# Constant-matrix multiplies on TensorE in three group normalisations and after the first attention

## The chip, the cores and the metric

One core of a Trainium2 chip runs the whole program. The metric is the device time of one execution in microseconds (us), the median of several executions. The engines are TensorE (PE, with its weight loads as PEld), VectorE (DVE), ScalarE (ACT), GpSimd (POOL) and SyncE (SP), which issues the transfers.

## The reference

The input is 8 samples of 256 channels by 32 x 32 positions, in float32. Four blocks follow each other, each added to its input, and each after a group normalisation over 32 groups of channels:

```python
x = x + _L0_conv_ref(_gn(x), ...)   # projections, state-space scans over three resolutions, projection
x = x + _L1_conv_ref(_gn(x), ...)   # attention, 8 heads of 32, over 1024 positions
x = x + _L2_conv_ref(_gn(x), ...)   # dilated depthwise 3x3 convolutions, two 1x1 mixes
x = x + _L3_conv_ref(_gn(x), ...)   # channel norm, attention, channel norm, projection

def _gn(v, G=32, eps=1e-05):
    g = v.reshape(B_, G, C_ // G, H_, W_)
    m = jnp.mean(g, axis=(2, 3, 4), keepdims=True)
    s = jnp.var(g, axis=(2, 3, 4), keepdims=True)
    return ((g - m) / jnp.sqrt(s + eps)).reshape(v.shape)
```

## The kernel before

The kernel is written engine by engine: each engine has its own instruction list, in the order of the source, and semaphores tie the lists together. Nothing reorders them. The channels lie on the partitions in two halves; the 1024 positions are worked in chunks of 512, which fill one PSUM bank of float32 each. All eight banks are one tensor, `PS`.

The samples run one after the other in the loop at the end of the TensorE part. For each of them TensorE does `block0` (block 0, whose last matmuls are on line 1210), `group_norm(b, 1)`, `attention(b, 0)` (its last matmuls are on lines 1301 and 1311, sums of the softmax's rows), `project(b, 0)`, `group_norm(b, 2)`, `block2(b)` (it begins with the depthwise taps of line 1374), `group_norm(b, 3)`, `chan_norm(b, 0)` (channel means of line 1216, channel variances of line 1222), `attention(b, 1)`, and the rest of block 3. The fourth normalisation of a sample, of the next sample's input, is made by `norm_means(b, 4)` and `norm_variances(b, 4)` apart, within the last projection.

A group normalisation goes back and forth between three engines. VectorE takes statistics of each chunk as it is written (line 702) and sums them (line 714). TensorE multiplies the sums by the matrix `g8`, which averages over the 8 channels of a group, into two columns of bank 7 (line 1072). VectorE makes squares of deviations (lines 718 to 727). TensorE multiplies them by `g8` into two columns of bank 6 (line 1076). ScalarE takes logarithm and exponential (lines 429 and 431), VectorE makes the shift (line 731), and VectorE and ScalarE write one half of the normalised `xg` each (lines 734 and 434). TensorE waits for both halves before the next block begins. All these waits are in the TensorE list, so nothing stands in it beside them.

After the first attention TensorE waits for `o_sb(b, 4)`: ScalarE takes the reciprocals of the last rows' sums (lines 605 and 609), and VectorE writes the attention's last outputs into `oT` (lines 973 and 975). Then `linear` (line 1087) makes the projection. Line 1087 is the helper of nearly all 1x1 products, each 128x512 with a 128x128 weight.

A float32 `pe.matmul` shows as two pairs of weight load and MATMUL in the profile. So the 12 products that `attention` makes after a normalisation are 24 records.

`mean128` is a constant 128x128 matrix of 1/128, made once at the start. Bank 5 is in use in the blocks, and nothing in it is live in the normalisations or at the end of the first attention.

Of the kernel before, what the change touches and what calls it, by code (L numbers as in the profile page):

```python
# [23 lines left out]
P = 128  # L24
# [68 lines left out]
def build(nc, x, wpack, vpack, w8, out):  # L93
    with ExitStack() as ctx:
# [18 lines left out]
        mean128 = sb("mean128", [P, P])  # L113
# [23 lines left out]
        PS = ctx.enter_context(nc.psum_tensor("PS", [P, 8, N], F32))  # L137
# [925 lines left out]
        def _(pe):  # L1063
# [3 lines left out]
                pe.matmul(PS[:, s, 0:P], W8[:, s, 0, :], W8[:, s, 1, :], start=True, stop=True).then_inc(folded, 1)  # L1067
            pe.wait_ge(prepared, NPREP)

            def norm_means(b, s):  # L1070
                pe.wait_ge(*gn_sum(b, s + 1))
                pe.matmul(PS[:, 7, 0:2], g8[:, :], msum, start=True, stop=True).then_inc(gn_gm.sem, 1)

            def norm_variances(b, s):
                pe.wait_ge(*gn_m2(b, s + 1))
                pe.matmul(PS[:, 6, 0:2], g8[:, :], m2, start=True, stop=True).then_inc(gn_gv.sem, 1)

            def group_norm(b, s):
                norm_means(b, s)
                norm_variances(b, s)  # L1080
                pe.wait_ge(*gn_xa(b, s + 1))
                pe.wait_ge(*gn_xb(b, s + 1))

# [129 lines left out]
            def chan_norm(b, s, X):  # L1213
                for c in range(NC):
                    for t in range(CT):
                        ins = pe.matmul(PS[:, c, :], mean256[:, :], X[:, t, c * N:c * N + N], start=(t == 0), stop=(t == CT - 1))
                    ins.then_inc(cm_ps.sem, 1)
                for c in range(NC):
                    n = NC * s + c
                    pe.wait_ge(*cm_sq(b, 2 * n + 2))  # L1220
                    for t in range(CT):
                        ins = pe.matmul(PS[:, 2 + c, :], mean256[:, :], sq[:, 2 * c + t, :], start=(t == 0), stop=(t == CT - 1))
                    ins.then_inc(cv_ps.sem, 1)
# [130 lines left out]
            def project(b, a, X, between=None):  # L1354
                for m in range(CT):
                    for c in range(NC):
                        if a == 1 and m == 0:
                            chunk_ready(b, NC + c)
                        if between is not None and m == 0 and c == 1:
                            between()  # L1360
                        if m == 0 and c == 0:
                            pe.wait_ge(*o_raw(b, 4 * a + 4))
                        linear(2 * m + c, w_proj[a], m, X, c, o_ps)

            def block2(b):
                for t in range(2):
                    for c in range(NC):
                        n = 2 * t + c
                        top = c * (HH // NC)
                        for hh, (ky, kx), (y0, y1, x0, x1), first, last in windows(t, c):  # L1370
                            dy, dx = (ky - 1) * RATES[2 * t + hh], (kx - 1) * RATES[2 * t + hh]
                            dst = PS[64 * hh:64 * hh + 64, n, :].rearrange("p (h w) -> p h w", w=WW)[:, y0 - top:y1 - top, x0:x1]
                            src = xg[:, t, :].rearrange("p (h w) -> p h w", w=WW)[:, y0 + dy:y1 + dy, x0 + dx:x1 + dx]
                            ins = pe.matmul(dst, DW[:, t, ky * 3 + kx, 64 * hh:64 * hh + 64], src,  # L1374
                                            start=first, stop=last, skip_group_check=True)
                        ins.then_inc(dw_ps.sem, 1)
                for m in range(2):
                    for c in range(NC):
                        pe.wait_ge(*dw_sb(b, 4))
                        linear(4 + 2 * m + c, MX, m, br, c, mix_ps)  # L1380
                for m in range(2):
                    for c in range(NC):
                        pe.wait_ge(*mix_sb(b, 4))
                        linear(2 * m + c, w_o, m, zm, c, o_ps)

            group_norm(0, 0)
            for b in range(B):
                block0(b)
                group_norm(b, 1)
                attention(b, 0, xg)  # L1390
                pe.wait_ge(*o_sb(b, 4))
                project(b, 0, oT)
                group_norm(b, 2)
                block2(b)
                group_norm(b, 3)
                chan_norm(b, 0, xg)
                attention(b, 1, xg)
                pe.wait_ge(*o_sb(b, 8))
                chan_norm(b, 1, oT)
                norm_means(b, 4)  # L1400
                project(b, 1, oT, lambda: norm_variances(b, 4))
                pe.wait_ge(*gn_xa(b, 5))
                pe.wait_ge(*gn_xb(b, 5))
                pe.wait_ge(*x_new(b, 16))
# [120 lines left out]
```

## Time and profile before

| | |
|---|---|
| Median of 3 runs | 5492.75 us (5491.58 to 5498.53) |
| The profiled execution: its own time | 5495.14 us |
| The profiled execution: its span | 5493.3 us |
| Mean granted TensorE clock over the span | 0.853 |
| TensorE busy | 4249.1 us (77%) |
| VectorE busy | 3607.0 us (66%) |
| ScalarE busy | 2146.6 us (39%) |
| GpSimd busy | 2007.6 us (37%) |

The span runs from the first to the last instruction; 1.8 us of the execution lie outside it. The granted clock is the share of TensorE's full 2.4 GHz that the chip let through: 1.00 is 2.4 GHz, 0.50 is 1.2 GHz, and a number between them over a stretch is a mean of the two levels. A sample takes about 682 us, and the eight are alike but for the places where the clock changes.

### The profile page before, as it was taken

How to read it: one execution, taken by the hardware profiler on the slowest of the kernel's cores; microseconds unless marked ns; L12 is line 12 of the kernel's file. 1: busy time of each engine (PE TensorE's matmuls, PEld its weight loads, DVE VectorE, ACT ScalarE, POOL GpSimd, SP SyncE). 2: the span in 40 equal slices, each digit the busy share in tenths (PEclk: the TensorE clock that was granted, in tenths of full speed). 3: DMA queues.
4: the chain of work that ended last, by engine and by line, in shares of the span. 5: the costliest groups of instructions: out<-in, count | busy, mean ns of one | idle time of the engine just before them, and what ended most of it. 6: DMA issues, size and time to landing. Idle time of an engine off the chain costs nothing.

```text
span 5493.3 us, 44457 instructions
## 1 busy us (share of the span) xinstructions
PE 4249.1 (77%) x16298; PEld 1843.1 (34%) x16298; DVE 3607.0 (66%) x4793; ACT 2146.6 (39%) x2639; POOL 2007.6 (37%) x681
## 2 busy tenths in 40 slices
PE   5688866879668896688866878669796697866978
PEld 2243422434224332243322433224332243322333
DVE  6763677637776368764687646867468674686746
ACT  3233452334423354243542425424254242542524
POOL 3531435404344043440444504434044340443404
PEclk7689977999769997799977999779897798977999
DMA  0020100210002100022000120011200112001020
GB/s 36 0 55 19 29 8 7 48 29 19 8 8 47 34 14 8 9 47 44 3 8 14 41 46 1 8 25 30 46 1 8 31 24 46 1 8 29 19 46 9
DMA packets 62956, 125.75 MB, mean 23 GB/s; under 512 B 18825, under 2 KB 21001, under 8 KB 62482
## 3 DMA queue, kind: packets, MB, share of 16 engines
q1 hardware_dynamic: 62738, 122.91, 9.6%
q8 instruction: 129, 2.11, 0.2%
q14 instruction: 89, 0.73, 0.0%
HBM read 12.23 MB, written 8.39 MB: 4 GB/s over the span
## 4 chain that ended last, share of the span: by engine, by line
PE 47%; DVE 28%; issue 10%; ACT 7%; SPq 4%; POOL 2%; DMA 2%; DVEq 0%; ACTq 0%; POOLq 0%
DVE mx L954 9%; PE PS L1250 8%; PE PS L1292 8%; PE PS L1087 7%; PE PS L1340 7%; PE PS L1374 4%; DVE work L846 3%; DVE work L848 3%; PE PS L1146 3%; PE PS L1184 2%; ACT PT L624 2%; SPq L290 2%; PE PS L1301 2%; SPq L299 2%; POOL work L392 1%
## 5 line engine op out<-in xcount | busy, mean ns | idle before, releaser
L954 DVE TENSOR_REDUCE mx<-PS 128x1 f32<-128x512 f32 x2048 | 1338.1, 687 | 422.0 <-PE PS L1250 417.9
L624 ACT ACTIVATE PT<-PS 128x1024 f32<-128x1024 f32 x1024 | 1006.9, 1023 | 689.9 <-PE PS L1340 660.0
L1250 PE MATMUL PS<-KS,QS 96*128 96x512 f32 x2048 | 894.9, 479 | 195.4 <-DMA KS<-piece 84.7
L408 POOL TENSOR_TENSOR piece<-PT 128x2048 f32<-128x2048 f32 x48 | 220.0, 4584 | 2183.4 <-ACT PT L624 2183.4
L408 POOL TENSOR_TENSOR piece<-piece,PT 128x2048 f32<-128x2048 f32 x192 | 878.0, 4573 | 58.4 <-ACT PT L624 47.1
L388 POOL TENSOR_TENSOR work<-work,Crep 128x1024 f32<-128x1024 f32 x256 | 616.3, 2409 | 390.5 <-DVE work L846 193.1
L1340 PE MATMUL PS<-QS,KS 98*128 98x512 f32 x2048 | 681.4, 424 | 45.9 <-DMA QS<-nm 22.2
L1250 PEld LDWEIGHTS PS<-KS,QS 96*128 96x128 f32 x2048 | 378.0, 197 | 816.2 <-DVE mx L954 578.0
L1292 PE MATMUL PS<-PT,Vt 128*32 128x512 f32 x4096 | 546.0, 605 | 27.0 <-ACT PT L624 27.0
L1184 PE MATMUL PS<-dstk,sel 128*128 128x512 f32 (+1 forms) x640 | 315.7, 568 | 321.1 <-DVE work L848 133.0
L542 ACT ACTIVATE PS<-PS,Aneg 128x1024 f32<-128x1024 f32 x256 | 278.3, 1087 | 628.5 <-PE PS L1184 597.8
L1184 PE MATMUL PS<-ustk,sel 128*128 128x512 f32 (+1 forms) x640 | 335.3, 597 | 182.9 <-DVE work L831 85.6
L1340 PEld LDWEIGHTS PS<-QS,KS 98*128 98x128 f32 x2048 | 376.5, 197 | 291.0 <-ACT PT L624 164.5
L1087 PE MATMUL PS<-xg,W 128*128 128x512 f32 x640 | 354.0, 709 | 81.1 <-ACT Brep L470 36.3
L1184 PEld LDWEIGHTS PS<-dstk,sel 128*128 128x128 f32 x640 | 152.9, 268 | 460.5 <-DVE work L846 178.9
L1184 PEld LDWEIGHTS PS<-ustk,sel 128*128 128x128 f32 x640 | 139.7, 257 | 491.1 <-DVE work L831 170.5
L1146 PE MATMUL PS<-work,ysel 128*32 128x512 f32 (+1 forms) x1536 | 273.1, 802 | 39.3 <-POOL work L392 30.6
L831 DVE TENSOR_TENSOR work<-PS,Brep 128x1024 f32<-128x1024 f32 (+1 forms) x256 | 250.7, 979 | 71.7 <-PE PS L1184 68.8
L946 DVE SCALAR_TENSOR_TENSOR piece<-PS,V,piece 128x1024 fp32r<-128x1024 f32 x64 | 82.2, 1284 | 278.1 <-ACT piece L588 278.1
L392 POOL TENSOR_TENSOR work<-work,Crep 128x640 f32<-128x640 f32 x128 | 210.5, 1648 | 138.7 <-DVE work L857 80.4
L373 POOL TENSOR_TENSOR ustk<-work,ustk 64x1024 fp32r<-64x1024 f32 x16 | 37.6, 2352 | 587.9 <-ACT ustk L485 587.3
L1087 PEld LDWEIGHTS PS<-xg,W 128*128 128x128 f32 x640 | 144.7, 231 | 263.2 <-issue 182.6
(198 smaller groups left out, 4983.0 us busy)
## 6 DMA issues: line engine op xcount, KB each, us to landing
QS<-piece SPq DMA_DIRECT2D x384, 128.0 KB, 2.4
KS<-piece SPq DMA_DIRECT2D x384, 128.0 KB, 2.4
xin<-x SPq DMA_DIRECT2D x8, 1024.0 KB
out<-xr SPq DMA_DIRECT2D x8, 1024.0 KB, 4.0
W<-wpack SPq DMA_DIRECT2D x2, 1024.0 KB
QS<-nm SPq DMA_DIRECT2D x128, 8.0 KB, 1.9
W<-wpack SPq DMA_DIRECT2D x1, 576.0 KB
W<-wpack SPq DMA_DIRECT2D x2, 256.0 KB
```

Source lines behind the costliest of these rows:

```text
L388: pool.tensor_tensor(slot, h, Crep[:, at:at + L], ALU.mult).then_inc(hC_sb.sem, 1)
L392: pool.tensor_tensor(two(slot), two(h), Crep[:, None, at:at + W3].broadcast_to((P, 2, W3)), ALU.mult).then_inc(hC_sb.sem, 1)
L408: pool.tensor_tensor(total, first, PT[:, i % 3, :, :], ALU.add).then_inc(sum_pool.sem, 1)
L542: act.activation(dst, src, ACT.Exp, scale=Aneg[:, ps * SG + g:ps * SG + g + 1]).then_inc(dA_sb.sem, 1)
L624: act.activation(PT[:, i % 3, 2 * pr:2 * pr + 2, :], PS[:, 2 + 2 * pr:4 + 2 * pr, :], ACT.Exp, scale=SCALE).then_inc(p_sb.sem, 1)
L954: dve.tensor_reduce(mx[:, at, cc:cc + 1], PS[:, row_slot(n, cc), :], AX.X, ALU.max).then_inc(r_max.sem, 1)
L1087: ins = pe.matmul(PS[:, bank, :], w[:, k, m * P:m * P + P], X[:, k, c * N:c * N + N], start=(k == 0), stop=(k == CT - 1))
L1146: ins = pe.matmul(PS[32 * j:32 * j + 32, c, 0:N if ps < 2 else W3], ysel[:, q % 4, :], src, start=(q % 4 == 0), stop=(q % 4 == 3), skip_gr ...
L1184: ins = pe.matmul(PS[:, slot + c, 0:wc], sel[:, g % 8, :], stk[:, g // 8, at + c * N:at + c * N + wc], start=True, stop=True)
L1250: pe.matmul(PS[:, row_slot(n, cc), :], QS[0:kd, c, h, q * P:q * P + P], KS[0:kd, h, cc * N:cc * N + N], start=True, stop=True).then_inc(r_ ...
L1292: ins = pe.matmul(PS[32 * j:32 * j + 32, 0, :], Vt[:, kt, DH * h:DH * h + DH], PT[:, i % 3, j, :], start=(kt == 0), stop=(kt == KT - 1), s ...
L1340: ins = pe.matmul(PS[:, 2 + 2 * pr + jj, :], KS[:, h, kt * P:kt * P + P], QS[:, c, h, :], start=True, stop=True)
```

## The change

A helper `keep_busy(count)` issues so many products of `mean128` with itself, 128 columns each, into the first 128 columns of bank 5. Nothing reads them, they wait for nothing and signal nothing. `group_norm` calls it three times, for every normalisation but the very first one: 6 products ahead of the wait for the sums, 4 ahead of the wait for the squares, and 10 ahead of the wait for the normalised `xg`. In the loop over samples there are 18 between the first attention and the wait for its outputs. The loop calls `group_norm` for 1, 2 and 3, so a sample has 3 x 20 + 18 = 78 products, and the kernel 624. The normalisation made by `norm_means(b, 4)` and `norm_variances(b, 4)` has none.

```diff
+            def keep_busy(count):
+
+                for _ in range(count):
+                    pe.matmul(PS[:, 5, 0:P], mean128[:, :], mean128[:, :], start=True, stop=True)
+
...
             def group_norm(b, s):
+                if b + s > 0:
+                    keep_busy(6)
                 norm_means(b, s)
+                if b + s > 0:
+                    keep_busy(4)
                 norm_variances(b, s)
+                if b + s > 0:
+                    keep_busy(10)
                 pe.wait_ge(*gn_xa(b, s + 1))
                 pe.wait_ge(*gn_xb(b, s + 1))
...
                 attention(b, 0, xg)
+                keep_busy(18)
                 pe.wait_ge(*o_sb(b, 4))
                 project(b, 0, oT)
```

The other engines' lists are the same before and after. On TensorE, ahead of the first attention, the list before has the last products of block 0, the two small ones of the normalisation, and the attention's first projections:

```order
L1164 MATMUL PS<-work,mean 128x320 x2
L1210 MATMUL PS<-work,W 128x512 x4
L1072 MATMUL PS<-small,g 128x2
L1076 MATMUL PS<-small,g 128x2
L1087 MATMUL PS<-xg,W 128x512 x12
```

The changed list has at the same place (its lines are numbered 5 to 11 higher; 1073 is `keep_busy`, 1077 and 1081 are the two small products):

```order
L1175 MATMUL PS<-work,mean 128x320 x2
L1221 MATMUL PS<-work,W 128x512 x4
L1073 MATMUL PS<-mean 128x128 x6
L1077 MATMUL PS<-small,g 128x2
L1073 MATMUL PS<-mean 128x128 x4
L1081 MATMUL PS<-small,g 128x2
L1073 MATMUL PS<-mean 128x128 x10
L1098 MATMUL PS<-xg,W 128x512 x12
```

Twenty products now stand between block 0 and the attention, none of them past anything else. On TensorE at the end of the first attention and in the normalisation ahead of block 2, the list before is:

```order
L1311 MATMUL PS<-piece,ones 32x512 x4
L1087 MATMUL PS<-oT,W 128x512 x8
L1072 MATMUL PS<-small,g 128x2
L1076 MATMUL PS<-small,g 128x2
L1374 MATMUL PS<-xg,DW 64x512 x2
```

and the changed one is:

```order
L1322 MATMUL PS<-piece,ones 32x512 x4
L1073 MATMUL PS<-mean 128x128 x18
L1098 MATMUL PS<-oT,W 128x512 x8
L1073 MATMUL PS<-mean 128x128 x6
L1077 MATMUL PS<-small,g 128x2
L1073 MATMUL PS<-mean 128x128 x4
L1081 MATMUL PS<-small,g 128x2
L1073 MATMUL PS<-mean 128x128 x10
L1385 MATMUL PS<-xg,DW 64x512 x2
```

The eighteen stand ahead of the projection, and have to be through before it can begin.

## Rows read from the trace of the kernel before

**Rows 1.** The page's 40 equal slices: granted clock in tenths.
```profile
PEclk7689977999769997799977999779897798977999
```
**Rows 2.** The page's chain that ended last, by engine.
```profile
PE 47%; DVE 28%; issue 10%; ACT 7%; SPq 4%; POOL 2%; DMA 2%; DVEq 0%; ACTq 0%; POOLq 0%
```
**Rows 3.** The chain in order of time, sample 4, first normalisation: start us, us, what.
```profile
2323.24 1.25 ACT xg L434
2324.62 6.20 PE PS L1087 x8
2330.85 1.12 ACT piece L588
...
2333.30 0.69 SPq L290
```
**Rows 4.** The same chain at the third normalisation of that sample.
```profile
2559.58 6.48 PE PS L1216 x8
2566.08 0.70 DVE xg L927
```
**Rows 5.** TensorE in order of time, first normalisation; [idle before <- what ended it].
```profile
2315.79 2.01 PE L1210 MATMUL PS<-work,W 128*128 128x512 f32 x4
2320.73 0.38 PE L1072 MATMUL PS<-small,g 128*128 128x2 f32 x2 [2.94 <-DVE small L714]
2321.97 0.38 PE L1076 MATMUL PS<-small,g 128*128 128x2 f32 x2 [0.86 <-DVE small L727]
2324.62 1.19 PE L1087 MATMUL PS<-xg,W 128*128 128x512 f32 x1 [2.26 <-ACT xg L434]
```
**Rows 6.** The same view, means of the second and of the third normalisation.
```profile
2506.98 0.43 PE L1072 MATMUL PS<-small,g 128*128 128x2 f32 x2 [2.23 <-DVE small L714]
...
2555.27 0.59 PE L1072 MATMUL PS<-small,g 128*128 128x2 f32 x2 [2.99 <-DVE small L714]
```
**Rows 7.** Windows from the first product after normalisation 1: us, PE busy (records), clock, DMA.
```profile
2324.60:2332.60 8.00, 7.98 (x13) 0.68 0.05 6
...
5051.90:5059.90 8.00, 8.00 (x13) 0.68 0.03 3
```
**Rows 8.** The same windows after normalisation 2.
```profile
467.40:475.40 8.00, 7.98 (x28) 0.66 0.00 0
...
2511.10:2519.10 8.00, 7.98 (x34) 0.82 0.01 2
```
**Rows 9.** The same windows after normalisation 3.
```profile
516.90:524.90 8.00, 7.68 (x13) 0.77 0.00 0
...
2559.60:2567.60 8.00, 8.00 (x12) 0.65 0.00 0
```
**Rows 10.** The same windows from the first attention's projection.
```profile
454.20:462.20 8.00, 7.09 (x16) 1.00 0.00 0
...
2495.90:2503.90 8.00, 7.98 (x15) 0.79 0.00 1
```
**Rows 11.** Groups by line, busy us and mean ns: line 1216 after normalisation 3.
```profile
L1216 PE MATMUL PS<-xg,mean 128*128 128x512 f32 x8 | 6.5, 985 | 2.3 <-ACT xg L434 2.3
```
**Rows 12.** Line 1216 at the second attention's end, in the same view.
```profile
L1216 PE MATMUL PS<-oT,mean 128*128 128x512 f32 x8 | 3.7, 605 | 2.6 <-DVE oT L975 2.6
```
**Rows 13.** In order of time, the end of the first attention in sample 4.
```profile
2492.68 0.61 PE L1311 MATMUL PS<-piece,ones 128*32 128x512 f32 x4
...
2495.38 0.49 DVE L975 TENSOR_SCALAR oT<-oT,V 128x512 f32<-128x512 f32 x1
...
2495.92 0.70 PE L1087 MATMUL PS<-oT,W 128*128 128x512 f32 x1 [2.63 <-DVE oT L975]
```
**Rows 14.** TensorE in order of time: short products one behind the other, in block 0.
```profile
1411.44 1.00 PE L1117 MATMUL PS<-f,W 128*128 128x64 f32 x8
1412.28 1.07 PE L1102 MATMUL PS<-f,Wd 128*128 128x512 f32 x2
```
**Rows 15.** The same view, products of 256 columns in an attention.
```profile
2596.48 1.03 PE L1234 MATMUL PS<-W,xg 128*128 128x256 f32 x4
```
**Rows 16.** The same view, the program's first products.
```profile
15.62 1.65 PE L1067 MATMUL PS<-W 8*128 8x128 f32 x6 [15.62 <-DMA W<-wpack]
```

## The prediction, made before the changed kernel ran

> **What bounds the kernel now.** I read the page's slices first. The granted clock is full in few of the 40 slices, and dips again and again [rows 1]. Then the chain of waits: TensorE holds 47% of it, VectorE 28%, no transfer more than a few per cent [rows 2]. So TensorE's speed counts, but only where it stands on the chain. The third view is the chain in order of time at the four places that the change touches. After the first normalisation it goes from ScalarE's half of `xg` straight to TensorE's first eight records of line 1087, and from them over ScalarE and VectorE to SyncE's transfers [rows 3]. After the third one it runs through all eight records of line 1216 into VectorE [rows 4]. After the second one it runs through the depthwise taps. TensorE is the engine that is late at all of them, and whatever it gains there moves the end. In the gaps ahead of them it is idle: 2.94, 0.86 and 2.26 us [rows 5], 2.23 and 2.99 us ahead of the means of the other two [rows 6], 2.63 us at the attention's end [rows 13]. The fourth view, windows of 8 us from the first product after each gap, shows what follows. TensorE is busy for all 8 us, at a mean clock of 0.68, 0.66 to 0.82, and 0.65 to 0.77 [rows 7 to 9]. The clock fell to its 1.2 GHz level during the gap and came back to 2.4 GHz only after some microseconds of work.
>
> **What the slow stretches cost.** In such a window the time lost is (1 - clock) x 8 us, if all of it is TensorE's work.
> - Normalisation 1: the eight windows read 0.65 once and 0.68 or 0.69 seven times [rows 7]. Together 20.6 us.
> - Normalisation 2: four at 0.66 or 0.67, four at 0.79 to 0.82 [rows 8]. Together 17.1 us.
> - Normalisation 3: four at 0.77, four at 0.64 or 0.65 [rows 9]. Together 18.7 us. A second view agrees: line 1216 takes 6.5 us for its eight records here [rows 11], and 3.7 us at the end of the second attention, at the full clock [rows 12]. That is 2.8 us for the worse kind.
> - The attention's end: four of the eight at 0.79, four at 1.00 [rows 10]. Together 6.7 us.
> - The small products: means take 0.43 and 0.59 us where the clock is down against 0.38 us [rows 5, 6], variances the same way. I put 3 us for all of them.
>
> The first three come to 56.4 us, with the other two 66.1 us.
>
> **What a dummy product costs.** No product of 128 columns with a 128-wide weight at the full clock stands in the trace. The nearest rows are these. Eight records of 64 columns start 0.84 us ahead of the next line, so one takes 0.105 us, which must be the weight load, since its columns are half as many [rows 14]. Four records of 256 columns take 1.03 us with the tail of the last, some 0.215 us each [rows 15]. The six records of 128 columns at the start take 1.65 us, up to 0.275 us each, but with long weight loads as at the low clock [rows 16]. Since 512 columns cost 0.43 us and 256 cost 0.215, 128 columns should stream in 0.11 us, and load and stream overlap in the other rows. I take 0.11 us for a record and 0.22 us for a product, and keep 0.105 and 0.275 us as ends.
>
> **Where they lie.** TensorE can start one about 0.17 us ahead of the drawn end of the record before it. At the full clock:
> - Six take 1.3 us, inside 2.2 to 3.0 us of waiting for the statistics. They cost nothing; VectorE's line 702 and 714 cover them.
> - Four follow the means: 0.22 + 0.88 = 1.10 us, against 1.24 us from means to variances [rows 5]. Nothing, with 0.14 us to spare.
> - Ten follow the variances: 0.22 + 2.20 = 2.42 us against 2.65 us to the next line 1087 [rows 5]. Nothing, with 0.23 us to spare; the cover is ScalarE's and VectorE's writing of `xg`.
> - Eighteen take 3.96 us. The last records of line 1311 start at 2492.68, so TensorE is free at about 2493.11, and the projection began at 2495.92 [rows 13]. There are 2.81 us, and the eighteen overrun them by 1.15 us in every sample. The outputs are then ready, and what waits is `linear`, VectorE's residual behind it, and all the rest. 8 x 1.15 = 9.2 us lost, against the 6.7 us above.
>
> **Does the clock stay up?** Work in the gap is denser than before but not full: between the six and the means TensorE is idle for 1.6 us in normalisations 1 and 3, and for 0.9 us in normalisation 2. A window with 7.09 of 8 us busy holds 1.00 [rows 10], and the gaps are cut from 6.8 us with 0.8 us of work to about 2 us of idleness in sum. So I expect it to hold mostly. Where it falls all the same within the gap, most of the ten run at half speed: seven at 0.44 us in place of 0.22 us, 1.5 us more, of which 0.23 us are covered. The projections then start 1.3 us late, but the clock is up soon after, since TensorE has been working without a break. Such a gap gives back about 1.0 of 2.5 us. I count one in four of the 16 gaps of normalisations 1 and 3 this way: 4 x 1.5 = 6 us less.
>
> The Trainium skill speaks against so large an effect. In "TensorE: Matmul & The Clock Gate", Part 1 (The HAM clock gate), it says that for modelling the ramp penalty is under 1% of a typical kernel's span, which here would be a bound of 55 us on all clock terms. The rows give 63 us for the four places, and the measurement decides.
>
> **The sum.** 56.4 + 6.7 + 3.0 - 9.2 - 6.0 = 50.9 us less. The profiled execution would go from 5495.1 to 5444.2 us. It lies 2.4 us above the median of the three, so the median would be 5441.8, say 5442 us.
>
> What is late next: after normalisation 1 SyncE's transfers and VectorE's maxima, which both start earlier by the same amount; TensorE then waits as long as before for them. The clock falls again in that wait, so those slow stretches stay.
>
> **The rivals.**
> - *The clock falls anyway in most gaps of normalisations 1 and 3.* For it: the 1.6 us of idleness, and products of two columns that hardly occupy the engine. Against it: the ten dense ones at the end. Each of 16 gaps gives 1.0 us: 17.1 + 16 + 6.7 + 3 - 9.2 = 33.6 us less, 5459 us.
> - *The slow stretches move.* Every stretch after a gap shifts by some us, and falls of the clock elsewhere hit other work; the windows of normalisations 2 and 3 come in two kinds for that reason alone [rows 8, 9]. A swing of 1.5 to 2 us for a sample is 12 to 16 us in all, either way: 5426 to 5458 around the forecast. With the weaker hold at once, 5475 us.
> - *Load and stream don't overlap fully at 128 columns.* One record would be longer than 0.11 us. By the page just named, Part 2 (Back-to-back issue gap), a stream of load and matmul pairs of 128 columns has 81 ns for each; with two such passes in a record that would be an estimate of 0.16 us. A record of 0.16 us, halfway from 0.105 to 0.215 us, makes a product 0.32 us. The eighteen then overrun by 2.95 us, the ten by 0.77 us, the four by 0.26 us: 8 x 2.95 + 24 x 1.03 = 48 us lost, 18 us less in the end, 5475 us. Rows 14 speak against it.
> - *The dummies become the bound: slower.* Place: the end of each gap. A record of 0.215 us, as for 256 columns, gives 0.43 us a product: 4.9 us too late at the attention's end, 1.9 us after the variances, 0.7 us before them. 8 x 4.9 + 24 x 2.6 = 102 us lost against 66 us, 36 us slower, 5529 us. It decides from 0.178 us for a record on. The same side is reached if work on constant data into an unread bank doesn't hold the clock at all: the ten run mostly slow, 24 x 1.3 + 8 x 1.15 = 40 us slower, 5533 us. That is also the case in which the change doesn't do what it says.
>
> **How the numbers follow.** The forecast 0.58; the weak hold 0.17; slow stretches that move against the gain, or the 0.16 us record, 0.11; slower 0.10; no difference, by a mixture of these, 0.04. The range takes in the first two with their swing of about 16 us on either side: 5418 to 5476 us. A measurement of this kernel tells 0.2% (11 us) from no change: faster 0.86, same 0.04, slower 0.10.
>
> **What would show it.** In the changed profile the windows after the three normalisations should read close to 1.00, line 1216 should take 3.7 us in both places, and the small products 0.38 us. The 1210-to-1087 gap should stay at about 6.8 us in all. `keep_busy` should show 1248 records, 0.11 us apart. The projection after the first attention should start 1.15 us later, counted from the last record of the attention. I am wrong if the products stand more than 0.15 us apart, if the clock falls between the six and the means, or if the attention and scan stages lengthen by as much as the gaps' followers shrink.

## The result and the profile after

The changed kernel took 5444.4 us (median of 4 runs, 5441.9 to 5460.8) against 5493.5 us for the kernel before on the same chip: 49 us less by the medians. The ratio of the runs is 0.9917, 95% interval 0.9905 to 0.9929, so some 0.8% less. The profiled execution took 5446.4 us, with a span of 5444.7 us and a mean granted clock of 0.867, up from 0.853.

The slices and the chain of the page, to be laid beside [rows 1, 2]. TensorE's share of the chain has grown by a point, and line 1073, the dummy products, is now on the chain itself with 2%:

```profile
PEclk7799977999779997799977999779997799977999
...
PE 48%; DVE 28%; issue 10%; ACT 6%; SPq 4%; POOL 2%; DMA 2%; DVEq 0%; ACTq 0%; POOLq 0%
DVE mx L954 10%; PE PS L1261 8%; PE PS L1303 8%; PE PS L1098 7%; PE PS L1351 6%; PE PS L1385 3%; DVE work L846 3%; DVE work L848 3%; PE PS L1157 3%; ACT PT L624 2%; PE PS L1195 2%; PE PS L1073 2%; SPq L290 2%; PE PS L1312 2%; SPq L299 1%
```

TensorE in order of time at the first normalisation of sample 4, the place of [rows 5]. Lines 1077 and 1081 are the small products, 1098 is `linear`:

```profile
2303.09 1.50 PE L1073 MATMUL PS<-mean 128*128 128x128 f32 x12
2306.17 0.38 PE L1077 MATMUL PS<-small,g 128*128 128x2 f32 x2 [1.58 <-DVE small L714]
2306.42 1.14 PE L1073 MATMUL PS<-mean 128*128 128x128 f32 x8
2307.41 0.38 PE L1081 MATMUL PS<-small,g 128*128 128x2 f32 x2
2307.66 2.48 PE L1073 MATMUL PS<-mean 128*128 128x128 f32 x20
2310.07 3.24 PE L1098 MATMUL PS<-xg,W 128*128 128x512 f32 x7
```

From means to variances it is still 1.24 us, and from variances to the projection still 2.65 us: neither the four nor the ten delay anything here. What is left idle are the 1.58 us ahead of the means.

The windows of 8 us from the first product after a gap, for [rows 7 to 9] in their order, and for the projection of [rows 10]; the columns are as there:

```profile
2310.00:2318.00 8.00, 8.00 (x21) 1.00 0.12 17
5012.10:5020.10 8.00, 8.00 (x19) 1.00 0.10 17
467.10:475.10 8.00, 8.00 (x44) 1.00 0.00 0
2494.70:2502.70 8.00, 8.00 (x43) 1.00 0.00 0
513.70:521.70 8.00, 7.47 (x18) 1.00 0.00 0
2541.20:2549.20 8.00, 7.49 (x18) 1.00 0.00 0
...
2481.50:2489.50 8.00, 8.00 (x29) 1.00 0.01 3
```

All 24 windows behind a normalisation start and stay at 1.00 in this profile, and TensorE gets through 17 to 44 records in the time in which it made 12 to 34 before. Line 1227, which was 1216, shows it by the groups of lines, against [rows 11]:

```profile
L1227 PE MATMUL PS<-xg,mean 128*128 128x512 f32 x8 | 3.7, 601 | 0.0
```

In three of the 24 gaps the clock fell all the same, each time in a third normalisation. In sample 2, in order of time:

```profile
1181.52 0.38 PE L1081 MATMUL PS<-small,g 128*128 128x2 f32 x2
1181.76 4.10 PE L1073 MATMUL PS<-mean 128*128 128x128 f32 x20
1185.70 0.59 PE L1227 MATMUL PS<-xg,mean 128*128 128x512 f32 x1
```

The ten products take 4.10 us in place of 2.48, and the next line starts 4.18 us after the variances in place of 2.65, which is 1.5 us late. It then runs at the full clock. The clock did not fall in the idle 1.65 us ahead of the means but just behind the variances, within 0.2 us of the start of the ten (in windows, granted clock in the last but two column):

```profile
1181.00:1181.80 0.80, 0.80 (x9) 1.00 0.00 0
1182.00:1185.00 3.00, 3.00 (x16) 0.50 0.01 3
```

The end of the first attention, against [rows 13]:

```profile
2476.42 1.04 PE L1322 MATMUL PS<-piece,ones 128*32 128x512 f32 x8
2477.39 4.29 PE L1073 MATMUL PS<-mean 128*128 128x128 f32 x36
2481.51 1.02 PE L1098 MATMUL PS<-oT,W 128*128 128x512 f32 x2
```

From the drawn end of the attention's last record to the projection it is now 4.05 us, not 2.63, in all eight samples: the eighteen come out 1.42 us too late.

The time of each stretch, summed over the eight samples. A gap runs from the drawn end of the last record ahead of it to the first real product behind it. The last row has seven stretches, since the first sample's block 0 lies ahead of the first mark:

| stretch, us in all | before | changed | difference |
|---|---|---|---|
| gap of normalisation 1 | 54.7 | 54.1 | -0.6 |
| first attention | 1347.1 | 1331.2 | -15.9 |
| its end and the projection | 84.9 | 88.7 | +3.8 |
| gap of normalisation 2 | 49.9 | 49.0 | -0.9 |
| block 2 | 334.7 | 318.1 | -16.6 |
| gap of normalisation 3 | 57.5 | 59.7 | +2.2 |
| channel norm and second attention | 1434.6 | 1416.5 | -18.1 |
| its end, channel norm, means of the last normalisation | 90.6 | 93.9 | +3.3 |
| last projection, and block 0 of samples 2 to 8 | 1729.4 | 1727.7 | -1.7 |

With 4 us less outside these stretches, nearly all of it at the two ends of the program, this makes the 48.6 us between the spans. The 3.3 us at the second attention's end are a slow stretch that turned up in more places: the first eight channel products there take 3.7 us at the full clock, and 5.2 to 5.4 us in three samples of the kernel before and in six of the changed one.

### The profile page after: what moved, and what is told of

It reads as the page before. It is cut to its first block, busy times and chain, and to the rows that moved or that the text cites. A ratio compares the mean times of both kernels' runs of the same rounds, so it can differ in the third digit from the quotient of the medians.

```text
span 5444.7 us, 46953 instructions
## 1 busy us (share of the span) xinstructions
PE 4337.0 (80%) x17546; PEld 1966.3 (36%) x17546; DVE 3605.7 (66%) x4793; ACT 2146.4 (39%) x2639; POOL 2006.2 (37%) x681
## 4 chain that ended last, share of the span: by engine, by line
PE 48%; DVE 28%; issue 10%; ACT 6%; SPq 4%; POOL 2%; DMA 2%; DVEq 0%; ACTq 0%; POOLq 0%
DVE mx L954 10%; PE PS L1261 8%; PE PS L1303 8%; PE PS L1098 7%; PE PS L1351 6%; PE PS L1385 3%; DVE work L846 3%; DVE work L848 3%; PE PS L1157 3%; ACT PT L624 2%; PE PS L1195 2%; PE PS L1073 2%; SPq L290 2%; PE PS L1312 2%; SPq L299 1%
## 5 line engine op out<-in xcount | busy, mean ns | idle before, releaser
L408 POOL TENSOR_TENSOR piece<-piece,PT 128x2048 f32<-128x2048 f32 x192 | 877.6, 4571 | 59.9 <-ACT PT L624 48.6
L1098 PE MATMUL PS<-xg,W 128*128 128x512 f32 x640 | 338.7, 682 | 63.0 <-ACT Brep L470 36.3
```

The costliest lines, as they stand in the source:

```text
L408: pool.tensor_tensor(total, first, PT[:, i % 3, :, :], ALU.add).then_inc(sum_pool.sem, 1)
L1098: ins = pe.matmul(PS[:, bank, :], w[:, k, m * P:m * P + P], X[:, k, c * N:c * N + N], start=(k == 0), stop=(k == CT - 1))
```

## The experiments

Each diff is against the changed kernel, or against another experiment that it names. They ran in three groups of four, each on one chip together with the kernel before, which took 5496.0, 5491.6 and 5495.7 us there. The first group is the four under the first heading. The second is the ten alone, the longer first group, and the two with 22 products. The third is the six and four, the two that put everything together, and the products of 2 columns. Across groups only the ratios can be compared.

### What the eighteen are worth

The changed kernel again, without an edit.

> The changed kernel itself, run again beside the others. Theory: 5444 us, 0.991 of the kernel before, with the clock up over 21 of the 24 gaps. Rival: its gain hangs on how the clock's changes happen to fall in one execution; then its runs spread over 15 us or more and another profile shows another number of gaps held.

Measured: 5450.3 us (5445.5 to 5456.3), ratio 0.992 (0.9906 to 0.9933). In its profile six gaps fell, all in third normalisations, against three before. The level of the gain stands. The executions of this one kernel differ by 11 us here and by 19 us in the first measurement. Three more fallen gaps are 4.6 us of that; there is only one profile of each measurement, so what the rest is isn't shown. So both sentences of the expectation hold a part: the gain doesn't hang on chance, some microseconds of it do.

The normalisations alone:

```diff
-                keep_busy(18)
                 pe.wait_ge(*o_sb(b, 4))
```

> The eighteen products behind the first attention are left out, the three groups in the normalisations stay. Theory: the eighteen cost 1.42 us in each sample (11.4 us in all) and give back the 7 us of the slow projections, so this kernel is 4 us faster than the changed one, 5440 us, and the clock holds in the normalisations as before. Rival: the eighteen also carry the clock into what follows; then the projection's slow stretches come back in more than four samples and this kernel is slower than the changed one, about 5450 us.

Measured: 5443.9 us (5438.2 to 5446.9), ratio 0.9904 (0.9889 to 0.9919), 6.4 us less than the changed kernel beside it. The projection was slow in six of eight samples, more than the four of before, and seven third normalisations fell. The runs of the two overlap a little (5445.5 to 5446.9), and so do the intervals. At their place the eighteen cost about what they bring: the attention's end and the projection take 88.7 us in sum with them and 88.3 us without. That the projection is slow in six samples without them, and not in four, is what the rival says. The sum went with the theory, but not at this place: between the two profiles the attentions are 17 us shorter, and block 0 and the second attention's end 10 us longer, and these sums move as much without a reason that a run shows.

The eighteen alone:

```diff
             def group_norm(b, s):
-                if b + s > 0:
-                    keep_busy(6)
                 norm_means(b, s)
-                if b + s > 0:
-                    keep_busy(4)
                 norm_variances(b, s)
-                if b + s > 0:
-                    keep_busy(10)
```

> Only the eighteen products behind the first attention are there, none in the normalisations. Theory: 11.4 us lost and 7 us gained, so 4 us slower than the kernel before, 5497 us, with all 24 gaps of the normalisations followed by slow work as before. Rival: the eighteen alone bring part of the gain, 5480 us.

Measured: 5499.9 us (11 runs), ratio 1.001 (1.0001 to 1.0019). Slightly slower, by as much as expected: the attention's end and the projection take 88.7 us in place of 84.9. All of the gain comes from the normalisations.

Twelve in place of eighteen:

```diff
-                keep_busy(18)
+                keep_busy(12)
```

> Twelve products behind the first attention in place of eighteen: 12 x 0.224 = 2.7 us, which end within the 2.8 us of waiting. Theory: the projection starts no later than in the kernel before and still at the full clock in all eight samples: 11 us less than the changed kernel, 5433 us. Rival: with twelve the clock falls in some samples, 5438 to 5442 us.

Measured: 5431.8 us (5426.9 to 5432.8), ratio 0.9884 (0.987 to 0.9897). That is 18.5 us less than the changed kernel beside it, and the runs of the two don't touch. TensorE in order of time at the end of the first attention:

```profile
2464.47 1.04 PE L1322 MATMUL PS<-piece,ones 128*32 128x512 f32 x8
2465.44 2.94 PE L1073 MATMUL PS<-mean 128*128 128x128 f32 x24
2468.22 7.05 PE L1098 MATMUL PS<-oT,W 128*128 128x512 f32 x16
```

The projection starts 2.71 us after the drawn end of the attention's last record, in place of 4.05, and its sixteen records take 7.05 us in all eight samples. So 10.7 us of overrun go and nothing is given back. The rest of the 18.5 us is that only two third gaps fell in this profile, and spread between runs.

### Which part of a gap matters

Only the ten (and the eighteen):

```diff
             def group_norm(b, s):
-                if b + s > 0:
-                    keep_busy(6)
                 norm_means(b, s)
-                if b + s > 0:
-                    keep_busy(4)
                 norm_variances(b, s)
```

> Of the changed kernel the six and the four are left out; the ten ahead of the wait for xg and the eighteen behind the first attention stay. Theory: the six and the four are what holds the clock through the gap. Without them it falls as in the kernel before, within the gap or at its end, most of the ten run at half speed and delay the next block by up to 2 us, and part of the slow stretch is only moved into the ten: about 5475 us, 30 us slower than the changed kernel. Rival: the ten dense ones alone bring the clock up for what follows, whatever happened before; then 5448 to 5455 us.

Measured: 5508.5 us (5500.3 to 5511.2), ratio 1.0031 (1.0019 to 1.0042): slower than the kernel before, and far slower than either expectation. First normalisation of sample 4, in order of time, and the window behind it:

```profile
2327.16 0.38 PE L1077 MATMUL PS<-small,g 128*128 128x2 f32 x2 [2.92 <-DVE small L714]
2328.40 0.38 PE L1081 MATMUL PS<-small,g 128*128 128x2 f32 x2 [0.86 <-DVE small L727]
2328.64 4.01 PE L1073 MATMUL PS<-mean 128*128 128x128 f32 x20
2332.44 3.75 PE L1094 MATMUL PS<-xg,W 128*128 128x512 f32 x8
...
2332.40:2340.40 8.00, 8.00 (x21) 0.98 0.07 12
```

The mechanism is the one expected. The clock falls in all 24 gaps and the ten run mostly at half speed. Behind the first normalisation the projection starts 1.4 us late and then runs at 0.98, and locally that is still a gain: the 24 records take 10.6 us, not 13.1. But the sum of the first attention fell by only 9.4 us for 19.6 us saved at its start, and the gap had lost 11.4 us; block 2 fell by 13.5 us and its gap lost 16.4; the second attention fell by 5.7 us and its gap lost 9.6. So in block 2 the faster start came back in full, and lost against a longer delay of 2 us a sample in its gap; in the two attentions it came back in part, as far as their sums can tell, which differ by 11 us among profiles of kernels that fill all gaps. Some 4 us of the whole are the eighteen's.

Only the six and the four (and the eighteen):

```diff
                 norm_variances(b, s)
-                if b + s > 0:
-                    keep_busy(10)
```

> The changed kernel without the ten products ahead of the wait for xg; the six, the four and the eighteen stay. Theory: the last 2.65 us of a gap are idle again, the clock falls at the end of some half of the 24 gaps and the next block then begins slowly: 5465 to 5475 us. Rival: six and four are enough, 5444 us, or better, since nothing is left that can overrun the gap.

Measured: 5494.2 us (11 runs), ratio 0.9994 (0.9985 to 1.0002), beside 5495.7 us for the kernel before: no difference. It ran in the last group. First normalisation of sample 4 and the windows behind normalisations 1 and 2:

```profile
2320.57 1.14 PE L1073 MATMUL PS<-mean 128*128 128x128 f32 x8
2321.57 0.38 PE L1081 MATMUL PS<-small,g 128*128 128x2 f32 x2
2324.22 3.75 PE L1096 MATMUL PS<-xg,W 128*128 128x512 f32 x4 [2.27 <-ACT xg L434]
...
2324.20:2332.20 8.00, 7.98 (x13) 0.68 0.06 6
2513.20:2521.20 8.00, 7.98 (x34) 0.79 0.00 0
```

The 2.27 us of idleness at the end are enough to lose the clock. It is down when the projection starts, and 0.68 is the very number of [rows 7]. All eight first gaps and all eight third gaps fell. The second gaps are another case. In two of them the clock fell in the last 0.2 us, and in six it was full to the end and fell 0.4 to 0.9 us behind block 2's first product, with TensorE at work again. In sample 4, the gap and a stretch 0.5 us behind its end:

```profile
2507.10:2513.20 6.10, 2.95 (x24) 1.00 0.00 0
2513.70:2516.70 3.00, 3.00 (x12) 0.50 0.00 0
```

Against the kernel before the ten alone cost 17 us, the six and four alone gain 1.5 us, and the whole gains 46 to 49 us, each with the eighteen, which cost 4. So neither part does it without the other. A piece of 1.6 us between the six and the means may stay idle, as in the changed kernel.

The first group made longer, on the kernel with twelve:

```diff
-                    keep_busy(6)
+                    keep_busy((0, 12, 9, 12)[s])
```

> Twelve products behind the first attention, and the group ahead of the means has 12, 9 and 12 products in normalisations 1, 2 and 3 in place of 6. 12 x 0.224 = 2.7 us end within the 2.9 us of waiting. Theory: the idle 1.65 us ahead of the means is where the clock is lost in the third normalisation; with it filled all 24 gaps hold, and each one that fell before gives 1.5 us back: 3 to 10 us less than with six, 5425 us. Rival: the falls come from the low load of the whole gap, and two or more of the third normalisations still fall: 5430 us.

Measured: 5433.2 us (5424.9 to 5443.5), ratio 0.9898 (0.9883 to 0.9912). The mechanism came out: none of the 24 gaps fell. The time didn't: it is that of the kernel with six. Its gap 3 was 55.1 us in sum against 57.9, and its attentions took 16 us more. The two profiles, of single executions on different chips, can't say whether that is the price of the filled gap or the spread of the attentions.

### Does it matter where TensorE is on the chain

22 products at the end of block 0, on the kernel with twelve; the first lines of the projection there were slow in every sample of the kernel before:

```diff
+                for _ in range(22):
+                    pe.matmul(PS[:, 2, 0:P], mean128[:, :], mean128[:, :], start=True, stop=True)
                 pe.wait_ge(*gated(b, 1))
```

> The kernel with twelve behind the first attention, and 22 products more at the end of block 0, ahead of the wait for the gated product, where TensorE idles for 6.65 us and the eight records of the output projection then begin at the low clock for 3.8 us. Theory: they hold the clock there and the projection gets 1.9 us shorter in each sample, 15 us in all: 5417 us. Rival: the clock is at its low level when they begin, so they take up to 9.8 us, overrun the gap by up to 3 us and make the kernel up to 25 us slower, 5457 us.

Measured: 5420.8 us (5419.7 to 5427.8), ratio 0.9877 (0.9862 to 0.9892), 10 and 12 us under the two other kernels with twelve beside it. The kernel with twelve alone didn't run in this group; by the ratios, 0.9877 and 0.9884, it is 4 us slower, and the intervals overlap. The end of block 0 in sample 4, in order of time:

```profile
2278.25 1.87 PE L1175 MATMUL PS<-work,mean 128*128 128x320 f32 x4
2279.96 5.07 PE L1219 MATMUL PS<-mean 128*128 128x128 f32 x44
2287.02 3.70 PE L1223 MATMUL PS<-work,W 128*128 128x512 f32 x8 [1.99 <-DVE work L909]
```

The eight records take 3.70 us in place of 5.58 (the PE busy time in the kernel before's window from 2312.2). Six of the eight first gaps fell now, which had all held, and took 1.4 us back each. So of 15 us saved some 8.5 us were lost again, which leaves 6 to 7 us.

22 products ahead of the first row scores of each attention, on the kernel with twelve:

```diff
+                keep_busy(22)
                 for n in range(PHASE_ROWS):
                     for cc in range(NC):
                         row_scores(n, cc)
```

> The kernel with twelve behind the first attention, and 22 products more in each attention between the first projections and the first row scores, where TensorE waits 5.2 us for transfers and then runs 3 to 6 us at the low clock. Theory: the chain of waits goes there over SyncE's transfers and VectorE's maxima, so TensorE is not late; the clock comes up at this place and the time stays within 4 us of 5432 us. Rival: each slow stretch after a gap costs half its length, as in the normalisations; then 16 x 2 = 32 us less, 5400 us.

Measured: 5431.3 us (5428.1 to 5441.3), ratio 0.9896 (0.9883 to 0.991), beside 0.9884 (0.987 to 0.9897) for the kernel with twelve: no gain, and the 32 us of the rival are out. TensorE in order of time in sample 4, and the window of 20 us that begins 12 us after the attention's first projection, first this kernel:

```profile
2312.83 5.07 PE L1073 MATMUL PS<-mean 128*128 128x128 f32 x44
2318.26 0.70 PE L1261 MATMUL PS<-KS,QS 96*128 96x512 f32 x2 [0.36 <-DMA KS<-piece]
...
2314.50:2334.50 20.00, 17.89 (x84) 1.00 0.94 205
```

and the kernel with twelve without them:

```profile
2314.91 1.19 PE L1261 MATMUL PS<-KS,QS 96*128 96x512 f32 x2 [5.24 <-DMA KS<-piece]
2315.90 3.56 PE L1098 MATMUL PS<-xg,W 128*128 128x512 f32 x4
...
2311.10:2331.10 20.00, 15.12 (x49) 0.83 0.90 196
```

This profile has the highest mean clock of all the kernels, 0.876, and no gain from it: its attentions take 2748 us in sum, those of the kernel with twelve 2737. TensorE waits there for transfers, and the chain of [rows 3] goes over these. It is the clearest sign in the runs that clock is only worth having where TensorE is on the chain.

All of it together, and with twelve behind the second attention too:

```diff
-                    keep_busy(6)
+                    keep_busy((0, 12, 9, 12)[s])
...
+                for _ in range(22):
+                    pe.matmul(PS[:, 2, 0:P], mean128[:, :], mean128[:, :], start=True, stop=True)
                 pe.wait_ge(*gated(b, 1))
...
-                keep_busy(18)
+                keep_busy(12)
...
+                keep_busy(12)
                 pe.wait_ge(*o_sb(b, 8))
```

(The last addition is only in the second of the two kernels.)

> All that helped so far: 12, 9 and 12 products ahead of the means of the three normalisations, 4 and 10 as in the changed kernel, 12 behind the first attention, 22 at the end of block 0. In the kernel with 22 at the end of block 0 alone the clock fell in six of eight first gaps and in two third gaps, at 1.5 us each. Theory: those eight hold now, 12 us less than 5421 us: 5409 us. Rival: the slow stretches only move to other places, as they seem to have done where the first group was made longer alone; then 5416 to 5421 us.

> The same, with 12 products behind the second attention too, where two to five samples had 1.2 us of slow channel means. Theory: 2 to 6 us less than without them, 5405 us. Rival: no difference.

Measured: 5422.2 us (5418.2 to 5429.0), ratio 0.9868 (0.9853 to 0.9883), and 5420.1 us (5416.8 to 5423.9), ratio 0.9861 (0.9847 to 0.9874). In both profiles all 24 gaps hold. The rival was right: closing the last eight fallen gaps brought nothing that can be told from the spread over the 22 products alone (0.9868 and 0.9877, on two chips). The twelve behind the second attention brought 2 us, within the spread too, though the channel products there, slow in two samples without them, were fast in all eight. By the ratios these are the fastest kernels of the study, 1.3% and 1.4% under the kernel before and some 0.5% under the changed one; the kernel with the 22 products alone can't be told from them.

### Columns or instructions

All 624 products 2 columns wide:

```diff
-                    pe.matmul(PS[:, 5, 0:P], mean128[:, :], mean128[:, :], start=True, stop=True)
+                    pe.matmul(PS[:, 5, 0:2], mean128[:, :], mean128[:, 0:2], start=True, stop=True)
```

> The changed kernel with all 624 products 2 columns wide in place of 128, with the same weight loads. Theory: it is the columns streamed that hold the clock; with two of them TensorE works as good as nothing, the clock falls in nearly all 24 gaps as in the kernel before, and what is left is the cost of the weight loads, 5500 to 5515 us. Rival: any instruction on TensorE holds it; then 5440 to 5450 us.

Measured: 5550.5 us (5545.9 to 5554.0), ratio 1.0097 (1.0083 to 1.0111). First normalisation of sample 4, in order of time, and the window behind it:

```profile
2349.24 1.03 PE L1073 MATMUL PS<-mean 128*128 128x2 f32 x8
2350.24 0.38 PE L1081 MATMUL PS<-small,g 128*128 128x2 f32 x2
2350.48 3.81 PE L1073 MATMUL PS<-mean 128*128 128x2 f32 x20
2354.15 4.28 PE L1098 MATMUL PS<-xg,W 128*128 128x512 f32 x5
...
2354.20:2362.20 8.00, 8.00 (x16) 0.76 0.02 2
```

The eight records behind the means take 1.03 us, nearly the 1.14 us of 128 columns, so the dummies cost what they did. But the clock falls, in all 24 gaps, the ten become 3.81 us, the projection starts late and is still slow. TensorE is drawn as busy in the profile all this time; with two columns at a time that doesn't hold the clock. The time is 35 us beyond the expectation's upper end, since here both losses come together, late and slow. The gaps are 45 us longer in sum than in the kernel before, the first attention's end and the projection, slow in all eight samples, 21 us, and the stretches behind the gaps only 14 us shorter.

## Why the prediction was right

The forecast was 5442 us, the measurement 5444, and the mechanism and the large terms of the sum behind it held up. That the two agree to 2 us is partly luck: single executions spread over 19 us, and beside it in the second measurement the same kernel was 46 us faster than the kernel before, not 51. And terms that nobody forecast cancelled others. By the profiles, 50.6 us came from the stretches behind the gaps for a forecast of 56.4, -3.8 from the attention's end and the projection for -2.5, and -0.7 from the gaps for -3.0 (3.0 from the small products less 6.0 for the gaps that fall; they were 3.9 and 4.6). The second attention's end lost 3.3 us, and the last projections, block 0 and the program's ends gained 6 us, of which the sum had nothing.

- **The price of a dummy.** 0.11 us for a record was taken; they start 0.111 to 0.112 us apart. The two rivals that rested on a longer record are out. The Trainium skill, in "TensorE: Matmul & The Clock Gate", Part 2 (Back-to-back issue gap), gives 81 ns for a pair of load and matmul at 128 columns, which was made an estimate of 0.16 us for a record; the trace does not agree with that estimate for float32.
- **The slow stretches.** 56.4 us were put behind the three normalisations. The stretches behind the gaps became 15.9, 16.6 and 18.1 us shorter, 50.6 in all, in this profile. Normalisations 2 and 3 came back nearly in full (17.1 and 18.7 expected). For the second that is firm: block 2 takes 318.1 us in sum in this profile and in the eight others with all three groups. The sums of the attentions move. In those eight the first takes 1325.0 to 1335.8 us and the second 1408.1 to 1419.8, so that the second's gain is anything from 15 to 27 us, and its nearness to 18.7 is luck. The first normalisation did not come back in full here: its 24 records fell from 13.1 to 10.5 us in every sample, 20 us in all as reckoned, and the attention as a whole by 15.9. The rest went some 40 us later, in the first attention's later part. In samples 2, 5 and 6 nothing went, and the attention is 2.8 us shorter; the other five are 1.2 to 2.3 us shorter. Sample 4, 20 us from 39 us after the projections began, in the kernel before and in the changed one:

```profile
2363.60:2383.60 20.00, 14.42 (x49) 0.74 0.10 21
```

```profile
2349.10:2369.10 20.00, 15.05 (x49) 0.66 0.01 2
```

  The mean clock there went from 0.74 to 0.66, as in samples 1 and 3 (0.70 in sample 8, 0.74 as before in the others): a slow stretch that was in the kernel before too and is longer now. That is the rival of slow stretches that move, as a side term of 4 to 5 us. Why this one got longer isn't shown by any run.
- **The gaps that fall anyway.** Four of sixteen were put at 1.5 us each. It was three, or six in the second profile, at 1.5 us each. They were all in the third normalisation and none in the first, although the idle time ahead of the means is nearly the same, 1.65 and 1.58 us. So the idle length that the prediction argued with doesn't decide it alone. The three samples whose third gap fell, 2, 5 and 6, are the three whose first attention was shortest; whether that is the cause isn't shown. In none of them did it fall between the six and the means, which the prediction had named as a sign against it. With 22 products at the end of block 0 it turned round, and six first gaps fell beside two third ones.
- **A partly held gap.** The prediction gave such a gap 1.0 of 2.5 us as a net gain. At the gap itself that is right for the first normalisation, and the kernel with the ten alone shows it in seven of eight samples: 1.4 us late, 2.4 us gained. In the end result it is wrong. That kernel is 17 us slower than the one before, some 4 of them by the eighteen. The weak-hold rival, 5459 us, was thus priced too well. It didn't matter, because the gaps held.
- **The eighteen.** 9.2 us of loss were expected, and 11.4 came: the first dummy starts 0.11 us later than reckoned, and from it to the projection it is 4.12 us, not 3.96. The gain, 7.6 us, was put at 6.7. The sign of this term was right and its size nearly. With six products less its loss goes and its gain stays, and the prediction's own numbers would have shown it.
- **The bound of 55 us for all clock terms** was worked out from the rule on the ramp penalty in the Trainium skill, "TensorE: Matmul & The Clock Gate", Part 1 (The HAM clock gate). The page says it of the slow matmuls at a kernel's start; the prediction stretched it to every slow stretch. So stretched, it holds for the changed kernel (49 us) and not for the kernel with more such products: 0.9861 is 76 us.

The range of 5418 to 5476 us took in every single run of the changed kernel, the slowest being 5461.

## What to carry to other kernels

Where TensorE is on the chain right behind a wait of some microseconds, read the granted clock of the stretch after the wait: (1 - clock) x its length is what there is to win, and products of real width, at both ends of the wait and with no more than a small piece idle between them (with 0.9 to 1.6 us the clock held in 18 to 21 of 24 gaps here), win most of it. Count them to end before the wait does, at the full clock, and leave a margin: 1.4 us too many in one place cost a quarter of the whole gain here, and half-filled waits were worth nothing or less. Don't fill waits in which TensorE isn't late afterwards. And read the next gap too: a filled one can move the fall of the clock to another.

## What the runs showed of the hardware

- Two columns and 128 columns cost TensorE nearly the same with a 128-wide float32 weight: eight records in 1.03 and in 1.14 us, their starts 0.112 us apart in both. But with 128 the clock held in 18 to 21 of 24 gaps, and with two it fell in all 24.
- With the same work in the gap but for its last 2.3 us, all eight first gaps lost the clock, and seven of the windows behind them read 0.68 as in the kernel before. With those 2.3 us filled, all eight held.
- The clock can fall when TensorE is at work again: up to 0.9 us behind block 2's first product in the kernel without the ten, and within 0.2 us of the start of the ten in the three gaps of the changed kernel.
- The changed kernel moved by 11 and by 19 us between executions on one chip, and its two profiles show three and six of 24 gaps falling. The Trainium skill says in the same Part 1 of "TensorE: Matmul & The Clock Gate", of the slow matmuls at a kernel's start, that their number varies from run to run; no run here looks at the start, but the gaps vary in the same way.
